# PE's order inside a quad of both attentions: weights' turn before the last K turn, aggregation before the score products

## The reference

```python
q = ((x @ Wq[l].T + bq[l]) * scaling).reshape(n, H, DH)
k = (x @ Wk[l].T).reshape(n, H, DH)
v = (x @ Wv[l].T).reshape(n, H, DH)
scores = jnp.einsum('ehd,ehd->eh', q[tgt], k[srcidx])
m = jax.ops.segment_max(scores, tgt, num_segments=n)
p = jnp.exp(scores - m[tgt])
s = jax.ops.segment_sum(p, tgt, num_segments=n)
w = p / (s[tgt] + 1e-16)
agg = jax.ops.segment_sum(w[:, :, None] * v[srcidx], tgt, num_segments=n)
...
```

## Time and profile before

| | us |
|---|---|
| median of 3 runs | 3532.81 |
| lowest, highest | 3515.78, 3536.16 |
| the profiled execution, its time | 3550.72 |
| its span, first to last instruction | 3549.0 |
| attention of layer 0, about | 521 to 1435 |
| attention of layer 1, about | 1905 to 2796 |
| mean granted TensorE clock | 0.920 of full speed |

### The profile page before, as it was taken

How to read it: one execution, slowest core, us unless ns; L and a number is a source line. 1 busy time by engine, 2 the same in 40 slices (tenths; PEclk the granted TensorE clock), 3 DMA queues, 4 the chain that set the end, 5 groups by cost and what they waited for, 6 DMA issues and landing times.

```text
span 3549.0 us, 77563 instructions
## 1 busy us (share of the span) xinstructions
PE 2887.4 (81%) x32206; PEld 2211.4 (62%) x32206; DVE 1685.6 (47%) x3316; ACT 1281.2 (36%) x3625; POOL 1138.1 (32%) x1109
## 2 busy tenths in 40 slices
PE   6999978888888888586996777777777678589999
PEld 5877866666667766373875666666666564344444
DVE  4247764444444444556133333333333646565554
ACT  3324434444444444222322444444444312222221
POOL 0000015555555555000013655655655100211100
PEclk8999989999999999798997989989998899699999
DMA  6531037788877887320234777777777422111100
GB/s 217 222 127 63 31 128 254 259 268 270 269 261 259 275 271 262 87 84 6 98 145 172 261 260 266 263 261 264 262 264 257 120 85 63 36 48 36 36 26 26
DMA packets 223586, 608.79 MB, mean 172 GB/s; under 512 B 37008, under 2 KB 43792, under 8 KB 223219
## 3 DMA queue, kind: packets, MB, share of 16 engines
q0 software_dynamic: 137088, 466.78, 39.4%
q1 hardware_dynamic: 86131, 136.85, 11.5%
HBM read 525.96 MB, written 103.29 MB: 177 GB/s over the span
## 4 chain that ended last, share of the span: by engine, by line
PE 77%; issue 11%; DVE 7%; DMA 2%; ACT 2%; another core or an unknown queue 1%; POOL 1%; SPq 0%; DVEq 0%; POOLq 0%; ACTq 0%
PE ps L1160 12%; PE ps L1202 9%; PE ps L1190 6%; PE ps L2381 5%; PE ps L2402 4%; PE ps L556 4%; PE ps L557 4%; PE ps L558 4%; PE ps L1167 3%; PE ps L755 3%; PE ps L923 2%; PE ps L925 2%; PE ps L924 2%; PE ps L1846 1%; PE ps L1152 1%
## 5 line engine op out<-in xcount | busy, mean ns | idle before, releaser
L1077 POOL DMA_INDIRECT Y<-KVd,srcE x449 | 461.0, 1027 | 368.8 <-PE ps L1202 231.6
L1258 DVE TENSOR_REDUCE stage<-ps 128x4 f32<-128x512 f32 x208 | 143.9, 692 | 628.1 <-remote 516.2
L1202 PE MATMUL ps<-Y,G 128*32 128x64 f32 x7184 | 241.1, 224 | 166.6 <-issue 162.6
L1327 ACT ACTIVATE work<-ps 128x512 f32<-128x512 f32 x309 | 179.1, 597 | 494.1 <-PE ps L1160 485.3
L1327 ACT ACTIVATE G<-ps 128x512 f32<-128x512 f32 x315 | 183.1, 598 | 435.9 <-PE ps L1160 396.8
L1077 POOL DMA_INDIRECT WA<-KVd,srcE x186 | 190.6, 1025 | 416.6 <-PE ps L558 266.4
L1202 PEld LDWEIGHTS ps<-Y,G 128*32 128x32 f32 x7184 | 183.7, 111 | 214.8 <-issue 209.9
L1346 ACT ACTIVATE stage<-ps,stage 128x128 f32<-128x128 f32 x832 | 294.7, 366 | 32.7 <-PE ps L1167 23.8
L1160 PE MATMUL ps<-ident,Y 128*128 128x128 f32 x1796 | 272.5, 312 | 5.5 <-issue 4.7
L556 PE MATMUL ps<-Wh,xs 128*128 128x512 f32 x600 | 238.7, 398 | 37.0 <-DVE xs L496 37.0
L1160 PEld LDWEIGHTS ps<-ident,Y 128*128 128x128 f32 x1796 | 242.2, 163 | 31.6 <-issue 23.5
(11 more groups left out here) (345 smaller groups left out, 6534.0 us busy)
## 6 DMA issues: line engine op xcount, KB each, us to landing
KVd<-stage SPq DMA_DIRECT2D x96, 256.0 KB, 2.0
aggd<-work SPq DMA_DIRECT2D x6, 2048.0 KB, 7.4
Qd<-stage SPq DMA_DIRECT2D x48, 256.0 KB, 2.0
G<-aggd SPq DMA_DIRECT2D x48, 256.0 KB, 2.7
Y<-KVd,srcE POOLq DMA_INDIRECT x449
Y<-in_x SPq DMA_DIRECT2D x4, 1536.0 KB, 14.9
G<-mixq SPq DMA_DIRECT2D x24, 256.0 KB
mixd<-rowsb SPq DMA_DIRECT2D x24, 256.0 KB
```

The lines of the kernel that those rows point to most:

```text
L1077: pool.indirect_dma_start(out=kvs[a], out_offset=None, in_=KVd[l][:, :], in_offset=bass.IndirectOffsetOnAxis(ap=srcE[:, n:n + 1], axis=0)) ...
L1202: mm = pe.matmul(AG[32 * i:32 * i + 32, DH * h:DH * (h + 1)], probs[x][:, i, h, :], kvs[a][:, D + DH * h:D + DH * (h + 1)], start=(x == 0 ...
L1327: act.activation(kT[n % len(kT)], banks(l)[place_of(l, "k", n) % len(banks(l))][:, :], ACT.Copy).then_inc(out_a, 1)
```

## The change

Inside a quad PE now does three K turns, the weights' turn, the fourth K turn, the slot table's or queries' turn, the masks, the aggregation of the quad two before, and last the sixteen score products. The turn table follows, and with it the banks and counts. DVE copies out the weights before the slot table. No instruction comes or goes.

```diff
@@ turn_table
             for g in range(NQ + AGG_AT):
                 b, x = divmod(g, 2)
-                order += [("k", n) for n in range(4 * g + LOOK[l], 4 * g + LOOK[l] + 4) if n < ET]
+                order += [("k", n) for n in range(4 * g + LOOK[l], 4 * g + LOOK[l] + 3) if n < ET]
+                if g >= AGG_AT:
+                    order.append(("p", g - AGG_AT))
+                order += [("k", n) for n in (4 * g + LOOK[l] + 3,) if n < ET]
                 if x == 0 and b + 2 < NJ:
                     order.append(("hot", b + 2))
                 if x == 1 and b + 1 < NJ:
                     order.append(("q", b + 1))
-                if g >= AGG_AT:
-                    order.append(("p", g - AGG_AT))
@@ attend_pe
                 for i in range(4):
+                    if i == 3 and g >= AGG_AT:
+                        turn_p(g - AGG_AT)
                     if 4 * g + LOOK[l] + i < ET:
                         turn_k(4 * g + LOOK[l] + i)
...
                     turn_q(b + 1)
-                if g >= AGG_AT:
-                    turn_p(g - AGG_AT)
                 next(side, None)
                 if g < NQ:
                     masks(g)
+                if g >= AGG_AT:
+                    gather(g - AGG_AT)
+                if g < NQ:
                     for i in range(4):
                         score(4 * g + i)
-                if g >= AGG_AT:
-                    gather(g - AGG_AT)
                 next(side, None)
@@ attend_dve
                 next(side, None)
+                if g >= AGG_AT:
+                    empty_p(g - AGG_AT)
                 if x == 0 and b + 2 < NJ:
                     empty_hot(l, b + 2)
-                if g >= AGG_AT:
-                    empty_p(g - AGG_AT)
```

## The result

The changed kernel took **3807.27 us** (median of 4 runs, 3794.62 to 3816.10), the kernel before beside it 3533.28: ratio **1.0781**, interval 1.0747 to 1.0815. The forecast was 3488 with a range of 3435 to 3620.

A forecast was written before the change was run, and what follows sets the result against it. The prediction took a loop to bound the kernel: aggregation ends, POOL issues five DMAs, PE comes free for the remaining products and aggregation. Terms -59 + 14 = -45 us, from 3532.8 to 3488 us, range 3435 to 3620.

The forecast's parts named there:

- the loop: Per quad: aggregation ends, POOL issues five DMAs (6.4 us), PE finishes products and aggregation (1.0 us); cycle 8.55 us.
- the hold: In the attentions: PE's dense small matmuls are held up while POOL issues, free about 0.9 us after its last issue.
- Rival C: No change: PE's standing time comes from something counting instructions or time, such as instruction supply; 3505 to 3550 us, chance 0.21.
- Step 1: Products behind the aggregation: 0.3 us less at each of some 197 POOL waits for the aggregation, 59 us less.
- Rival B: Slower: products behind the aggregation run into POOL's new issues and are held; about +160 us, 3690 us, chance 0.27.
- Step 2: Weights' turn before the last K turn: PE waits 0.2 to 0.4 us a quad for DVE's weights, hidden; nothing charged.
- Step 3: Turn banks in layer 0's attention: the last K turn waits for DVE's copy, 0.13 us x 104 = 14 us charged.
- Step 4: DVE's copy of the weights before the hot copy: delays covered by PE work and POOL's queue; nothing charged.
- Step 5: POOL and DMA: same issues, fetches start as before, the later store of sums hidden in POOL's queue; nothing charged.

The follow-up runs named there:

- session Q: Sessions in which the unchanged kernel before takes 3.20 ms; four of the six sets of experiments fell in it.
- session P: Sessions in which the unchanged kernel before takes 3.53 ms; the first result and two of the six sets of experiments fell in it.

## Why the prediction was wrong

**The bound.** The forecast rested on the loop "POOL's last issue, then 0.9 us, then PE free". It is refuted twice: after the change the products come free while POOL issues, and in session Q POOL issues through them. What is right of it: with the K/V fetches gone the hold is nearly gone (5.12 us a quad against 8.55, both in session P). Rival C in its plain form falls with the same run: the kernel without fetches has its instructions in 262 packets against 263, and PE's chain has hardly a gap. The rule of "Runtime: NRT & Kernel Launch" in the Trainium skill, section Instruction fetch mechanics, that instruction fetch is mostly hidden, agrees with that run. What stands for a mixture of the two, that row fetches slow the supply in a run of small matmuls, is that the pause moved ahead of the products when 40 matmuls were put there; no run tests it.

**Step 1, the failed one (-59 us).** The swap alone lost 300 us in session P (1.0839) and 75 to 79 in session Q. The step took the hold to end in the aggregation, with a little of it and of the products behind the release, and counted 0.3 us a quad as won by moving the products away. By the semaphores the hold lay in the products, and the whole aggregation, 0.80 us, followed it; and nothing was set against the gain for the products in their new place. There both were held: from the last turn to the end of products and aggregation 5.62 us instead of 4.38 in attention 0, 5.46 instead of 5.17 in attention 1. Rival B described the signs: products held behind the aggregation, the minimum more than 2 us late, idle time moved before the turns. It had the chance 0.27 and a price of 160 us. Its hold was too large (4.3 us to the products' end; 3.06 measured), and it has the weights' turn wait for the late weights, which in session P were ready before PE had done its K turns. Its cycles were short all the same, 8.5 to 9 us in attention 1 (9.08 measured) and 10 in attention 0 (10.70): it left out that the aggregation is held too and that PE takes 2.8 to 3.1 us for three K turns behind the products.

Of attention 0's 198 us some 130 lie in the stretch of products and aggregation and some 75 in the turns (1.24 and 0.73 us in 103 quads, the sum a little over as these quads are not all). The runs without fetches split it otherwise: 52 us appear without fetches, so about 146 only with them. In attention 1 the 55 us are no more than the pair without fetches shows, 99, so no growth of the hold is needed there.

**Step 2 (0 us).** The wait of 0.2 to 0.4 us was sized rightly for a PE that is not held, and hidden behind a bound that wasn't one. Without fetches the changed order costs 0.5 us a quad in attention 0 and 0.5 (session Q) to 1.0 (P) in attention 1. In attention 1 a part is this wait and a part DVE's queue ahead of the weights' copy (copy of the sums 0.68 and ordering 0.28 in one quad of two, K copy 0.68), which the step left out. With the fetches, in session P, the wait did not occur. The place of the weights' turn is worth nothing either way by itself (1.0027 and 1.0005); beside the swap it gives back 0.6% in session P and 1.0 to 1.6% in session Q.

**Step 3 (+14).** The turn alone cost attention 0 14 us in one profile each of session Q, the size forecast, but within what two profiles differ by, so the match may be luck. **Step 4 (0)** is not separable from it. **Step 5 (0)** held for the store; but POOL's query fetch now waits for the query turn behind the last K turn, 278.0 us by the page.

**What stays open.** Why the same program runs with a hold in one session and without in another, and whether the issuing, the transfers or a supply that they slow holds PE in session P. Before the change the hold takes 3.4 us a quad there in attention 1 (8.55 less the 5.12 without fetches), and 1.8 in attention 0. Why it takes 3.2 in attention 0 after the change (10.70 less 7.49), where attention 1 has 3.0 (9.08 less 6.09), wasn't found; how much of it is the lower clock neither.

## What to carry to other kernels

When work is moved behind a point that lets something else go, follow the result of the moved work to its last reader, through every engine's queue, and ask what holds it in its new place. Where PE's records are dense, date its work by the semaphores or by the start of the engine that waits, before a pause is put down to one line: here that moves the pause from the aggregation to the products, and shows a wait for DVE that wasn't one. A bound inferred from "it ends 0.9 us after that" is a coincidence until a run without "that" exists; a small wait hidden by such a bound should be priced as if the bound were gone.

## What the runs showed of the hardware

- The same kernel took 3193 to 3200 us in four sets of runs and 3532 to 3539 in the others. The difference lies in the two attentions, the stretches with four row fetches a quad; the rest is the same within 20 us.
- In session P the products' end, as DVE sees it, comes 3 us after the aggregation, at 2311.67, while PE's records of the three K turns behind them already run from 2309.39 to 2311.27: a record's start on PE in a dense run of small matmuls is no proof that it ran then. The consumer's start is.
- In session P, with row fetches running, PE pauses in a run of small matmuls. The pause moves with the run and not with a line: in attention 1 between products before the change (2.20 us in the median), in aggregation and products after it, and ahead of the products where 40 matmuls were put there.
- 2.3 us of extra PE work ahead of the products cost the old order 1.0 to 1.1 us a quad; in attention 1, 0.7 of what doesn't show came with a granted clock of 0.97 instead of 0.89.
- POOL issues a fetch of 128 rows every 1.25 us, 0.94 of it busy; with rows of 256 bytes instead of 4096 its records took 0.97 each all the same.
